# Two attentions' query and key parts subtracted in PSUM by TensorE, three maxima beside the last projection chunks, and the grouped experts' first tokens loaded ahead of a batch

## The reference

```python
xn = _layernorm(x); x = x + _L0_attn_ref(xn, ...) + _L0_ffn_ref(xn, ...)   # selective scan; routed experts
xn = _layernorm(x); x = x + _L1_attn_ref(xn, ...) + _L1_ffn_ref(xn, ...)   # causal attention; 9 gated experts, top 2
xn = _layernorm(x); x = x + _L2_attn_ref(xn, ...) + _L2_ffn_ref(xn, ...)   # full attention; 8 experts, fixed token runs
xn = _layernorm(x); x = x + _L3_attn_ref(xn, ...) + _L3_ffn_ref(xn, ...)   # squared-relu gated attention; top-1 experts
```

```python
q = proj(Wq, bq); k = proj(Wk, bk); v = proj(Wv, bv)            # x @ W.T + b, by heads
scores = jnp.einsum('bhqd,bhkd->bhqk', q, k) * scale            # causal in the second layer
p = softmax(scores); out = jnp.einsum('bhqk,bhkd->bhqd', p, v) @ Wo.T + bo
h = silu(x @ w1[e].T) * (x @ w3[e].T); out += cw[:, e] * (h @ w2[e].T)   # grouped experts
```

## Time and profile before

| | us |
|---|---|
| median of 3 runs | 1759.99 (1756.71 to 1765.4) |
| the profiled execution | 1773.61, span of its profile 1771.7 |
| TensorE busy | 1478.0 (83%) |
| VectorE busy | 1240.8 (70%) |
| ScalarE busy | 938.7 (53%) |
| POOL busy | 795.9 (45%) |

### The profile page before, as it was taken

One profiled execution on the slowest core, in us unless ns is written; L12 is line 12 of the kernel. 1 busy time (PEld: TensorE's weight loads), 2 busy tenths in 40 slices (PEclk: granted clock), 3 DMA queues, 4 the chain that ended last, 5 costly groups with the idle time before them and its releaser, 6 DMA issues. The chain is left out here.

```text
span 1771.7 us, 31308 instructions
## 1 busy us (share of the span) xinstructions
PE 1478.0 (83%) x11180; PEld 918.3 (52%) x11180; DVE 1240.8 (70%) x2002; ACT 938.7 (53%) x1674; POOL 795.9 (45%) x722
## 2 busy tenths in 40 slices
PE   5994698898887866588799999964899999878997
PEld 5671244344343336255577766631345444556885
DVE  7655999999999977856455567658742899565335
ACT  1235577777775742545344456634654777533442
POOL 1487888778886743674144443123300000046341
PEclk9997999999999995789899999976899999789999
DMA  4523887778668936754322246207621342221223
GB/s 145 161 71 78 201 192 178 193 166 201 182 156 190 213 80 249 223 96 87 51 60 56 55 81 103 34 9 196 94 51 48 46 66 39 98 73 51 85 76 101
DMA packets 193559, 200.89 MB, mean 113 GB/s; under 512 B 22474, under 2 KB 142569, under 8 KB 193152
## 3 DMA queue, kind: packets, MB, share of 16 engines
q1 hardware_dynamic: 181816, 177.33, 42.3%
q0 software_dynamic: 11520, 21.52, 4.5%
q10 hardware_dynamic: 72, 0.03, 0.0%
HBM read 144.45 MB, written 57.48 MB: 114 GB/s over the span
## 5 line engine op out<-in xcount | busy, mean ns | idle before, releaser
L799 POOL TENSOR_TENSOR xn_t<-scan_b_rows,scan_du 128x1024 f32<-128x1024 f32 x128 | 307.1, 2405 | 86.6 <-DMA scan_b_rows<-states 55.6
L829 PE MATMUL banks<-scan_hc,ident 128*128 128x512 f32 x512 | 262.8, 625 | 78.5 <-DVE scan_hc L1013 78.0
L1005 DVE TENSOR_TENSOR_SCAN banks<-banks,xn_t 128x1024 f32<-128x1024 f32 x128 | 293.1, 2290 | 25.7 <-POOL xn_t L799 14.7
L2482 ACT ACTIVATE att_pr<-banks 128x768 f32<-128x768 f32 (+1 forms) x256 | 234.2, 916 | 135.4 <-PE banks L2374 80.5
L829 PEld LDWEIGHTS banks<-scan_hc,ident 128*128 128x128 f32 x512 | 88.9, 193 | 212.5 <-DVE scan_hc L1013 147.9
L934 ACT ACTIVATE banks<-delta,scan_exp_centre,a_neg 128x510 f32<-128x510 f32 x256 | 189.2, 770 | 0.3
L2527 DVE TENSOR_REDUCE att_mb<-banks 128x4 f32<-128x1024 f32 x128 | 153.9, 1222 | 21.3 <-PE banks L2341 16.3
L2523 DVE TENSOR_REDUCE att_mb<-banks 128x6 f32<-128x768 f32 x128 | 121.5, 956 | 56.6 <-PE banks L2348 43.2
L2390 PE MATMUL banks<-att_pr,att_vx 128*32 128x256 f32 (+1 forms) x2048 | 154.2, 373 | 7.1 <-ACT att_ot L2487 5.2
L1013 DVE TENSOR_TENSOR scan_hc<-banks,scan_c_rows 128x1024 f32<-128x1024 f32 x128 | 156.5, 1222 | 3.8
L2341 PE MATMUL banks<-att_ks,att_qs 48*128 48x256 bf16 (+1 forms) x1024 | 112.3, 276 | 38.2 <-DMA att_ks<-k_parts 31.6
(11 more groups left out here) (394 smaller groups left out, 3175.7 us busy)
## 6 DMA issues: line engine op xcount, KB each, us to landing
scan_b_rows<-states SPq DMA_DIRECT2D x128, 256.0 KB
scan_c_rows<-states SPq DMA_DIRECT2D x128, 256.0 KB, 5.0
scan_ew<-f_packed SPq DMA_DIRECT2D x12, 578.0 KB
q_parts<-att_p_parts SPq DMA_DIRECT2D x16, 384.0 KB
k_parts<-att_p_parts SPq DMA_DIRECT2D x16, 384.0 KB
att_qs<-q_parts SPq DMA_DIRECT2D x64, 96.0 KB
att_ks<-k_parts SPq DMA_DIRECT2D x64, 96.0 KB
disp<-blank_rows SPq DMA_DIRECT2D x1, 4680.0 KB, 15.0
```

Source lines behind the costliest of these rows:

```text
L799: nc.gpsimd.tensor_tensor(bu[:, q % AHEAD], b_rows[:, q % HELD, None, :].to_broadcast([P, DC, TT]), du[:, b % 2], ALU.mult).then_inc(s.bu_ ...
L829: nc.tensor.matmul(g.ps[:, Y0 + c, :], g.ident[:], hc[:, q % RING, c], start=False, stop=(q % DS == DS - 1)).then_inc(s.sum_done, 1)
L1005: v.tensor_tensor_scan(states, states, rows(bu[:, q % AHEAD]), 0.0, ALU.mult, ALU.add).then_inc(s.scan_done, 1)
L2482: nc.scalar.activation(pr[:, i % RING], g.ps[:, at:at + 2, 0:W], ACT.Exp, scale=scale).then_inc(s.p_ready, 1)
```

## The change

The projections keep a chunk's products in PSUM. VectorE (queries) and ScalarE (keys) each read the product with its bias three times and write the high, the middle and the low part as bf16; between the readings TensorE subtracts the part just written, multiplied by a negative identity matrix in bf16 (`neg_b`, new in `setup`), from the bank. The fp32 buffers in SBUF go. Chunks rotate through three pairs of banks; low parts are signalled apart for queries and keys. `EARLY` is 1: the halves of batches 0 and 1 stand behind the stores of chunks 1 to 4.

The first three maxima are issued inside the projections' last three turns of the loop, on TensorE (`maximum`) and on VectorE (`reduce`), all in banks 6 and 7, each waiting for the reduction of the one before. The turn of batch 0's maxima moves ahead of the maximum of pair 8. In SP's queue the grouped experts' first tokens move ahead of the wait for the last scores and of batch 9's loads, and the dense experts' weights move behind the row of maxima of batch 3.

```diff
@@ setup @@
-            for b, v in ((g.ident, 0.0), (g.ident_b, 0.0), (g.ones_b, 1.0), (g.before, 0.0),
+            for b, v in ((g.ident, 0.0), (g.ident_b, 0.0), (g.neg_b, 0.0), (g.ones_b, 1.0), (g.before, 0.0),
...
-            for b in (g.ident, g.ident_b):
-                nc.gpsimd.affine_select(out=b[:], in_=b[:], compare_op=ALU.not_equal, fill=1.0, base=0,
+            for b, v in ((g.ident, 1.0), (g.ident_b, 1.0), (g.neg_b, -1.0)):
+                nc.gpsimd.affine_select(out=b[:], in_=b[:], compare_op=ALU.not_equal, fill=v, base=0,
@@ projections @@
-    EARLY, PB = 2, 4
-    y = sb("p_y", [P, 2, 2, CH])
-    rem = sb("p_rem", [P, 2, 2, CH])
+    EARLY, PB, BANKS = 1, 4, 3
     parts = sb("p_parts", [P, PB, 6, CH], BF16)
+    HIGH, MID, LOW = (0, 5), (1, 4), (2, 3)
+    def bank(ch, m):
+        return g.ps[:, 2 * (ch % BANKS) + m, :]
     def sync(sp):
         for ch in range(NCH):
-            sp.wait_ge(s.p_low, ch + 1)
-            for m, out in ((0, q_parts), (1, k_parts)):
+            for m, out, low in ((0, q_parts, s.p_low_q), (1, k_parts, s.p_low_k)):
+                sp.wait_ge(low, ch + 1)
                 sp.dma_start(out[:, :, ch * CH:(ch + 1) * CH].rearrange("a r t -> r a t"),
                              parts[:, ch % PB, 3 * m:3 * m + 3]).then_inc(stored[ch % PB], 16)
...
+    def tensor(pe, beside):
+        def product(ch, m):
...
+            if ch >= BANKS:
+                pe.wait_ge((s.p_low_q, s.p_low_k)[m], ch - BANKS + 1)
+            nc.tensor.matmul(bank(ch, m), w[:, m, :], g.xn_t[:, ch * CH:(ch + 1) * CH], start=True,
+                             stop=True).then_inc((s.p_yq, s.p_yk)[m], 1)
+        def subtract_high(ch):
...
+            for m, high, left in ((0, s.p_high_q, s.p_rem_q), (1, s.p_high_k, s.p_rem_k)):
+                pe.wait_ge(high, ch + 1)
+                nc.tensor.matmul(bank(ch, m), g.neg_b[:], parts[:, ch % PB, HIGH[m]], start=False,
+                                 stop=True, skip_group_check=True).then_inc(left, 1)
...
+        for ch in range(NCH + 2):
+            product(ch, 0)
+            subtract_mid(ch - 2)
+            product(ch, 1)
+            subtract_high(ch - 1)
+            if ch >= NCH - 1:
+                beside(ch - NCH + 1)
+    def vector(dve, beside):
+        def take(ch, ready, part, done):
...
+            dve.wait_ge(ready, ch + 1)
+            if part is HIGH and ch >= PB:
+                dve.wait_ge(stored[ch % PB], ch // PB * 32)
+            nc.vector.tensor_scalar(parts[:, ch % PB, part[0]], bank(ch, 0), b[:, 0:1], None, ALU.add).then_inc(done, 1)
+        for ch in range(NCH + 2):
+            take(ch, s.p_yq, HIGH, s.p_high_q)
+            take(ch - 2, s.p_last_q, LOW, s.p_low_q)
+            take(ch - 1, s.p_rem_q, MID, s.p_mid_q)
+            if ch >= NCH - 1:
+                beside(ch - NCH + 1)
...
+        for ch in range(NCH + 2):
+            take(ch - 2, s.p_last_k, LOW, s.p_low_k)
+            take(ch, s.p_yk, HIGH, s.p_high_k)
+            take(ch - 1, s.p_rem_k, MID, s.p_mid_k)
@@ attention @@
+    BESIDE = 3
...
-            return (2 * (i - LEAD) + 1) % 3
+            return 3 if i < BESIDE else (2 * (i - LEAD) + 1) % 3
...
-                    if b == 1 and dense:
+                    if b == 2 and dense:
                         job.weights(sp)
+                    if moe and (b + 1) * PAIRS == MID:
+                        job.first_tokens(sp)
                     if b + BUFS < BATCH:
                         sp.wait_ge(s.s_ready, (b + 1) * PAIRS)
                         load(b + BUFS)
-                    if moe and (b + 1) * PAIRS == MID:
-                        job.first_tokens(sp)
...
-                    elif i >= 3:
+                    elif 1 <= i < BESIDE:
+                        pe.wait_ge(s.m_taken, i)
+                    elif i >= 3 + BESIDE:
                         pe.wait_ge(s.m_taken, i - 2)
...
+                parts.tensor(pe, maximum)
...
-                    if step + LEAD < NP:
+                    if step + LEAD == PAIRS:
+                        turn_maximum(0)
+                    if BESIDE <= step + LEAD < NP:
                         maximum(step + LEAD)
...
+                parts.vector(dve, reduce)
...
-                    if step + LEAD < NP:
+                    if BESIDE <= step + LEAD < NP:
                         reduce(step + LEAD)
```

More of the change, by code:

```diff
@@ L2013, in all_stored @@
             chunk_stored(eng, ch)
-    def tensor(pe):
-        pe.wait_ge(s.p_w_in, 64)
[L2017 to L2026, removed]
@@ L2028, in vector @@
-    def vector(dve):
-        dve.wait_ge(s.p_w_in, 64)
[L2031 to L2041, removed]
-                dve.wait_ge(s.p_low, ch - 1)
-            nc.vector.tensor_tensor(rem[:, ch % 2], y[:, ch % 2], parts[:, ch % PB, 0:6:5],
-                                    ALU.subtract).then_inc(s.p_rem, 1)
-        def low(ch):
-            dve.wait_ge(s.p_mid, ch + 1)
-            nc.vector.tensor_tensor(parts[:, ch % PB, 2:4], rem[:, ch % 2], parts[:, ch % PB, 1:5:3],
-                                    ALU.subtract).then_inc(s.p_low, 1)
-        take(0)
-        for ch in range(NCH):
-            if ch + 1 < NCH:
-                take(ch + 1)
-            remainder(ch)
-            if ch >= 1:
-                low(ch - 1)
-        low(NCH - 1)
@@ L2060, in scalar, with subtract_mid @@
[L2060 to L2087 removed]
+    def tensor(pe, beside):
+        def product(ch, m):
+            if not 0 <= ch < NCH:
+                return
+            if ch >= BANKS:
[3 more added lines that the diff above has]
+        def subtract_high(ch):
+            if not 0 <= ch < NCH:
+                return
+            for m, high, left in ((0, s.p_high_q, s.p_rem_q), (1, s.p_high_k, s.p_rem_k)):
+                pe.wait_ge(high, ch + 1)
+                nc.tensor.matmul(bank(ch, m), g.neg_b[:], parts[:, ch % PB, HIGH[m]], start=False,
+                                 stop=True, skip_group_check=True).then_inc(left, 1)
+        def subtract_mid(ch):
+            if not 0 <= ch < NCH:
+                return
+            for m, mid, left in ((0, s.p_mid_q, s.p_last_q), (1, s.p_mid_k, s.p_last_k)):
+                pe.wait_ge(mid, ch + 1)
+                nc.tensor.matmul(bank(ch, m), g.neg_b[:], parts[:, ch % PB, MID[m]], start=False,
+                                 stop=True, skip_group_check=True).then_inc(left, 1)
+        pe.wait_ge(s.p_w_in, 64)
+        for ch in range(NCH + 2):
[5 more added lines that the diff above has]
+                beside(ch - NCH + 1)
+        pe.wait_ge(s.p_low_q, NCH)
+        pe.wait_ge(s.p_low_k, NCH)
@@ new lines, in scalar, with take @@
+    def scalar(act):
+        def take(ch, ready, part, done):
+            if not 0 <= ch < NCH:
+                return
+            act.wait_ge(ready, ch + 1)
+            if part is HIGH and ch >= PB:
+                act.wait_ge(stored[ch % PB], ch // PB * 32)
+            nc.scalar.activation(parts[:, ch % PB, part[1]], bank(ch, 1), ACT.Identity, bias=b[:, 1:2]).then_inc(done, 1)
+        act.wait_ge(s.p_w_in, 64)
+        for ch in range(NCH + 2):
+            take(ch - 2, s.p_last_k, LOW, s.p_low_k)
+            take(ch, s.p_yk, HIGH, s.p_high_k)
+            take(ch - 1, s.p_rem_k, MID, s.p_mid_k)
@@ L2323, in _ @@
             def _(pe):
-                parts.tensor(pe)
-                if causal:
-                    pe.wait_ge(s.consts, 15)
                 def maximum(i):
@@ L2462, in _ @@
                         turn_back(b - 1)
-                    if 0 <= b + 1 < BATCH and j == TURN:
+                    if 1 <= b + 1 < BATCH and j == TURN:
                         turn_maximum(b + 1)
@@ L2515, in _ @@
                 dve.wait_ge(s.w_in, 64)
-                parts.vector(dve)
                 def reduce(i):
```

44 lines of the change are left out of this document (14 added, 30 removed).

## The result

The changed kernel takes 1749.64 us (median of 6 runs, 1747.0 to 1754.9) against 1762.7 for the kernel before beside it: ratio 0.9937, 95% interval 0.9911 to 0.9963, or 11 us less (6.5 to 15.7). The forecast was 22 less: right in direction, and in time within the range, but the gain is a half to two thirds of the forecast. Two executions far from all others, 2972 us of "tokens only" and 1979 of the kernel before, are left out of the ratios.

A forecast was written before the change was run, and what follows sets the result against it. The prediction took TensorE's in-order program, idle at waits in four places, as the bound. Tokens 10, weights 6 and projections 6 gave 22 us, subtracted from the median 1759.99: 1738 us, range 1728 to 1752.

The forecast's parts named there:

- the tokens' term: Before the grouped experts: earlier token loads cut TensorE's 9.83 us stall, leaving about 0.7 for VectorE; 10 us (7 to 11).
- the 1.8 us for faster passes: Behind the tokens' stall: eight fp32 passes at the full clock take 2.5 us instead of 4.35, 1.8 saved.
- the step that takes stalls of one profiled execution: In the sum: the profile's stalls are waits a profile does not make, so all 22 us come off the median 1759.99.
- Rival (e): The tokens' wait stays in another form (register loads or scatters' landing), or a weights' stall stays: 1748 to 1752; chance 0.07.
- Weights, 6: Second attention, ahead of the dense experts: later weight loads remove the 4.25 us row wait, faster scores 1.5; 6 us (2 to 6.5).
- Projections, 6: Both attentions' openings: first scores come earlier, 3 us for each attention (-2 to 6), 6 for both.
- rival (b): Projections: chunk 7's buffer wait moves out, 2 us later in each attention; gain 12, 1748 us; chance 0.13.
- This is where the 5 us go: Projections: loads start 5 us earlier, but VectorE and ScalarE stand behind chunk 7's buffer wait, so that gain is lost.
- rival (a): The row of maxima does not wait for the backlog: stages gain only 1.4, sum 17.4, 1742.5 us; chance 0.19.
- Nothing: Setup: the added memset and select on POOL cost nothing, showing only if longer than 1.1 us.
- (d): Projections: TensorE becomes the bound at the slow clock, 1.2 GHz through the chunks; 19 us slower, 1779; chance 0.04.
- a granted clock of 0.50 beyond chunk 1: Projections: a sign listed as showing the forecast wrong, TensorE's clock at 0.50 after chunk 1.

The follow-up runs named there:

- tokens only: The kernel before with only the grouped experts' eight token loads issued ahead of batch 9's loads; ratio 0.9965 to the kernel before, 6.1 us less.
- the combination: The changed kernel with early register loads, six buffers for the parts, and batch 3's loads straight behind batch 2's; ratio 0.9831 to the kernel before, 1735.1 us.

## Why the prediction was right in direction and too large

The three groups of waits went as described, but each term of the sum was too large. Two steps failed: in the tokens' term the 1.8 us for faster passes, since the clock fell behind the register loads' 2.24 us as it had behind the stall, and in the sum the step that takes stalls of one profiled execution, itself 13.6 us above the median, off the median in full.

- **Tokens, 10.** This is the largest miss. The stage takes 94.0 with late tokens (three executions, the long one left out) and 87.0 with early ones (four): 7.0; timed alone 6.1. Of the working, the tokens' landing in time and VectorE's 0.7 (0.91 once bare) held. The register loads, taken at 0.9 between 0 and 1.8 on top of it, take 2.24 with VectorE's wait beside them: 1.33 more than the wait alone, so the idle time is 2.24 where the sum has 1.6. That is the small part. With 2.24 us idle the clock fell to 0.50 as before and the passes take 4.6 us in the mean of both groups, so the 1.8 for faster passes wasn't there. Rival (e) named the register loads as the form in which the wait might stay; 2.24 of the 9.83 us did.
- **Weights, 6.** Stage 4.3, alone 2.3, taken back 3.7. The wait went as the prediction put it; it was sized by the one execution at hand, 4.25 plus 1.5, where five executions have a mean of 3.5. "The stalls are waits of a few us that a profile does not make" is where the sum failed: this wait behind a queue of loads is 4.25 and 2.25 us in two executions of the same kernel, and 2.23 to 4.88 over the five.
- **Projections, 6.** 2.3 and 2.4 in the stages (means of four and five executions), 4.2 alone. Chunk period, first store and first load came out as forecast in the second attention. Chunk 7's buffer came free at T0+27.2 and T0+26.0 in the mean of four executions with the old projections, at T0+27.9 and T0+26.7 with the new (five): 0.7 later in each, a third of what rival (b) has. That T0+26.9 came so near the 26.7 is partly luck: chunk 3's stores went out at T0+19.7 instead of 20.4 and landed 7.2 us later instead of 6.3. The split wasn't 0.7 earlier in both (from the prediction's own terms, 13.7 less 13.1 and 0.2, it would be 0.4): TensorE turns the split maxima at T0+40.6 after 41.8 in the first attention and at T0+41.2 in both kernels in the second. "This is where the 5 us go" held: without the buffer waits the loads and the row take their place at once.
- **The row of maxima.** From its issue to the first scores the second attention takes 6.2 to 6.6 us in four executions with the old projections and 3.8 to 4.5 in five with the new: the 2.4 us gained there are the row's alone, as forecast, and rival (a), by which only the split gains, falls there. In the first attention it is 7.0 to 7.9 and 5.6 to 6.8. The forecast says the row stands behind the backlog, rival (a) that it doesn't. Neither in full: holding SP's loads halves its landing in the second attention, holding POOL's scatters takes 1.6 of its wait in the first, yet in the combination it lands with the share at 0.6 to 0.8 and the loads still running. Other queues slow it; it doesn't come out last. The Trainium skill (DMA: Bandwidth & Descriptors, "Queues, rings and completion order") has each DMA engine switch between queues packet by packet: the landing ahead of the backlog's end agrees, the 3.7 us that other queues' loads cost so small a row are more than the prediction read into that rule.
- **Nothing, and (d).** The setup doesn't show: the stage to the first attention's projections takes 704.2 to 706.7 in four executions with the old setup and 703.0 to 711.2 in thirteen with the new. Rival (d) didn't come: TensorE's clock was 1.00 from T0+6 to the wait for chunk 6 and fell to 0.50 only with that wait, for chunks 6 and 7. By the letter this meets the mark "a granted clock of 0.50 beyond chunk 1", but not by its cause: it was a wait that came before it.

In all 7.0 + 4.3 + 4.7 = 16.0 by the stages, 12.6 by the single timings, 11 and 15 by the whole. The 3 us between these sums aren't located; the stages without an edit differ by 1.2, -0.6 and 0.8 between the two kernels' means, and each timing is known to 4 or 5 us.

Left on the path, and not seen beforehand as a target: batch 3's load wait, some 7 us a stage with the slow clock behind it. It was in the trace of before at 3.06 us and stands in no step of the prediction.

## What to carry to other kernels

Before a stall is put into a sum, look what else stands between the waiting instruction and the engine's last one (register loads have no row of their own), and whether an idle time as long as the one that would be left was followed by the slow clock elsewhere in the trace (here the stalls cost their length and the slow stretch behind them). A wait behind a queue of loads differs from execution to execution: profile the same kernel twice before sizing it. And read every wait in the stretch before choosing: here batch 3's loads, in the same loop of SP's program as the lines that were moved, were worth more than any one of the three edits.

## What the runs showed of the hardware

Two register loads that read SBUF took TensorE 2.24 to 2.33 us in front of the first transposes, some 1.1 each if they are alike. An idle time of 2.24 or 2.33 us was followed by a granted clock of 0.50 for some 3 or 7 us in seven executions, one of 0.82 or 0.91 by 1.00 in five. The row of maxima, two small loads on ScalarE's queue, took at most 3.8 us or 7.5 from issue to landing, by what SP's queue held. And twelve executions of the kernel before on one chip spread over 16 us (1754.7 to 1770.7); one profiled execution was 9.7 longer than another in a single stage.
